# Second cross-attention: plain float32 matmuls, row maximum and sum on TensorE, another order of the batches

## The reference

```
x = x + tanh(g_xattn[0]) * L0_xattn(layernorm(x), ctx, ctx)
x = x + tanh(g_ffn[0])   * L0_ffn(layernorm(x))
x = x + tanh(g_xattn[1]) * L1_xattn(layernorm(x), ctx)
x = x + tanh(g_ffn[1])   * L1_ffn(layernorm(x))
```

```
Sim = (hc @ w1)[:, :, None] + (hq @ w2)[:, None, :] + einsum('bid,bjd->bij', hc * w3, hq) + b_sim
A = softmax(Sim, axis=2)
hq_hat = einsum('bij,bjd->bid', A, hq)
Batt = softmax(max(Sim, axis=2), axis=1)
hc_bar = einsum('bi,bid->bd', Batt, hc)[:, None, :]
feats = concatenate([hc, hq_hat, hc * hq_hat, hc * hc_bar], axis=-1)
out = feats @ W_qv + b_qv
```

## Time and profile before

| | us |
|---|---|
| median of 3 runs | 1298.6 |
| lowest, highest | 1297.71, 1306.02 |
| the profiled execution | 1298.1 |
| its span | 1296.2 |

### The profile page before, as it was taken

How to read it: one execution, slowest core, us unless ns; L and a number is a source line. 1 busy time by engine, 2 the same in 40 slices (tenths; PEclk the granted TensorE clock), 3 DMA queues, 4 the chain that set the end, 5 groups by cost and what they waited for, 6 DMA issues and landing times.

```text
span 1296.2 us, 22004 instructions
## 1 busy us (share of the span) xinstructions
PE 1076.1 (83%) x7088; PEld 931.2 (72%) x7088; DVE 869.5 (67%) x2028; ACT 508.4 (39%) x984; POOL 365.9 (28%) x391
## 2 busy tenths in 40 slices
PE   3478888697999999999999999835667998799930
PEld 3467777576888888888888888725567777588820
DVE  6779999967766776677667776755546567533323
ACT  5568888652333333333333333243232332122210
POOL 6345656432111111111001111142331222332235
PEclk9789999999999999999999999967887999899975
DMA  8920000010000000000000002110100520123224
GB/s 237 219 43 1 0 0 0 2 50 13 26 24 24 24 24 24 17 19 24 24 24 24 24 24 53 33 33 17 33 17 1 221 88 1 34 89 91 82 83 135
DMA packets 28388, 61.74 MB, mean 48 GB/s; under 512 B 4688, under 2 KB 13392, under 8 KB 28208
## 3 DMA queue, kind: packets, MB, share of 16 engines
q1 hardware_dynamic: 24928, 51.77, 13.3%
q0 software_dynamic: 3408, 9.31, 2.7%
HBM read 42.85 MB, written 9.31 MB: 40 GB/s over the span
## 4 chain that ended last, share of the span: by engine, by line
PE 63%; DVE 18%; issue 9%; POOL 3%; DMA 3%; ACT 2%; SPq 1%; DVEq 0%; POOLq 0%; ACTq 0%
PE bank L776 27%; PE bank L793 14%; PE bank L1153 6%; DVE ptl L570 3%; PE bank L1174 3%; DVE nmax L562 2%; PE bank L1091 2%; PE bank L380 2%; DMA yg<-y_rows,slot 1%; SPq L2077 1%; PE bank L1658 1%; POOL yg L1464 1%; DVE stats L681 1%; PE bank L1107 1%; DVE x L919 1%
## 5 line engine op out<-in xcount | busy, mean ns | idle before, releaser
L919 DVE SCALAR_TENSOR_TENSOR x<-bank,cw,x 128x256 f32<-128x256 f32 x528 | 218.1, 476 | 4.7 <-PE bank L793 4.7
L776 PE MATMUL bank<-xh,wh 128*128 128x512 f32 x528 | 207.8, 394 | 0.0
L776 PE MATMUL bank<-xl,wh 128*128 128x512 f32 x528 | 207.4, 393 | 0.0
L776 PE MATMUL bank<-xh,wl 128*128 128x512 f32 x528 | 206.0, 390 | 0.0
L995 POOL TENSOR_TENSOR wl<-wraw,wh 128x768 fp32r<-128x768 f32 x33 | 60.9, 1847 | 445.7 <-ACT wh L845 445.7
L865 ACT ACTIVATE hidh<-hid 128x512 fp32r<-128x512 f32 x132 | 83.4, 632 | 211.9 <-DVE hid L930 208.9
L793 PE MATMUL bank<-wh,hidh 128*128 128x256 f32 x528 | 150.4, 285 | 12.0 <-POOL hidl L1005 6.8
L793 PE MATMUL bank<-wh,hidl 128*128 128x256 f32 x528 | 150.5, 285 | 0.0
L793 PE MATMUL bank<-wl,hidh 128*128 128x256 f32 x528 | 150.5, 285 | 0.0
L936 DVE TENSOR_TENSOR hidl<-hid,hidh 128x512 fp32r<-128x512 f32 x124 | 85.9, 693 | 86.6 <-ACT hidh L865 86.6
L858 ACT ACTIVATE sil<-bank 128x512 f32<-128x512 f32 x132 | 79.0, 599 | 163.7 <-PE bank L776 163.7
(11 more groups left out here) (253 smaller groups left out, 2261.2 us busy)
## 6 DMA issues: line engine op xcount, KB each, us to landing
wraw<-in_w SPq DMA_DIRECT2D x37, 384.0 KB, 3.0
kst<-khl SPq DMA_DIRECT2D x32, 224.0 KB, 5.5
wres<-in_w SPq DMA_DIRECT2D x4, 1536.0 KB, 13.9
y_rows<-yb SPq DMA_DIRECT2D x39, 128.0 KB
x<-in_x SPq DMA_DIRECT2D x4, 512.0 KB, 6.2
craw<-in_ctxt SPq DMA_DIRECT2D x4, 512.0 KB, 4.2
traw<-in_ctx SPq DMA_DIRECT2D x4, 512.0 KB, 4.0
xn_rows<-xn SPq DMA_DIRECT2D x4, 512.0 KB, 11.6
```

The source lines that it names most:

```text
L776: mm = pe.matmul(o[:, :], wp[:, par, w], xp[:, c, b * SEQ:(b + 1) * SEQ], start=(n == 0), stop=(n == 5))
L919: op = nc.vector.scalar_tensor_tensor(out=x[:, t, :], in0=bank[4 + 2 * vp + j // 2][:, (j % 2) * DIM:(j % 2 + 1) * DIM], scalar=w, in1=x[: ...
```

## The change

It has four parts. First, the matmuls of the stage take float32 operands as they are: no high and low parts, a third of the matmuls, and ScalarE copies what comes out of PSUM once (`probs_copy`, `attended_copy`). Second, the two all-reduces go. The column of maxima is transposed by TensorE into one row (`maxima_row`), VectorE takes its maximum, and a matmul with a row of ones spreads it over the partitions (`maximum_spread`); a matmul with a matrix of ones makes the sum on all partitions (`sum_spread`). Third, the context and the tokens get two buffers each, the order of the steps on TensorE, ScalarE and VectorE is another one, and the output is made in halves of which each uses one bank. Fourth, the parameters and the routed weights get places in SBUF of which the stage uses none, and `load_routed1` issues the loads of `wres` before the stage.

```diff
--- before.py
+++ after.py
         def sync_a1(sp):
             sp.wait_ge(moe.up, 4 * NB0)
             for b in range(BATCH):
-                if b:
-                    sp.wait_ge(A["clo"], b)
-                sp.dma_start(craw[:, :, :], ctxt_in[:, :, b * SEQ:(b + 1) * SEQ]).then_inc(A["ctx_t"], 16)
-                if b:
-                    sp.wait_ge(A["tlo"], b)
-                sp.dma_start(traw[:, :, :], ctx_in[:, b * TPB:(b + 1) * TPB, :]).then_inc(A["ctx"], 16)
+                if b >= 2:
+                    sp.wait_ge(A["sim"], 4 * (b - 1))
+                sp.dma_start(craw[:, b % 2], ctxt_in[:, :, b * SEQ:(b + 1) * SEQ]).then_inc(A[f"ctx_t{b % 2}"], 16)
+                if b >= 2:
+                    sp.wait_ge(A["hq"], 2 * (b - 1))
+                sp.dma_start(traw[:, b % 2], ctx_in[:, b * TPB:(b + 1) * TPB, :]).then_inc(A[f"ctx{b % 2}"], 16)
...
             def scores(b, tiles):
...
                     for c in range(CH):
-                        for ap_, cp in ((aench, ctxh), (aench, ctxl), (aencl, ctxh)):
-                            mm = pe.matmul(bank[j % 2][:, :], ap_[:, c, j * P:(j + 1) * P], cp[:, c, :],
-                                           start=(k == 0), stop=(k == 5))
-                            k += 1
+                        mm = pe.matmul(bank[j % 2][:, :], aenc[:, b % 2, c, j * P:(j + 1) * P], craw[:, b % 2, c, :],
+                                       start=(c == 0), stop=(c == CH - 1))
                     mm.then_inc(A["sim"], 1)
...
+            def maxima_row(b):
+                pe.wait_ge(A["mx"], b + 1)
+                pe.wait_ge(A["enc"], min(2 * b + 4, 2 * BATCH))
+                pe.transpose(bank[3][0:1, 0:P], mx1[:, 0:1], ident).then_inc(A["mxt"], 1)
+
+            def maximum_spread(b):
+                pe.wait_ge(A["gmx"], b + 1)
+                pe.matmul(bank[3][:, P:P + 1], ones[0:1, :], gmx1[0:1, 0:1], start=True, stop=True).then_inc(A["gmb"], 1)
+
+            def sum_spread(b):
+                pe.wait_ge(A["eb"], b + 1)
+                pe.wait_ge(A["ngmx"], b + 1)
+                pe.matmul(bank[3][:, P + 1:P + 2], ones[:, :], ebs[:, 0:1], start=True, stop=True).then_inc(A["ebt"], 1)
...
             for b in range(BATCH):
-                probs_transposed(b, (0, 1))
                 if b + 1 < BATCH:
                     scores(b + 1, (0, 1))
+                if b == 0:
+                    maximum_spread(0)
+                probs_transposed(b, (0, 1))
+                if b == 0:
+                    sum_spread(0)
                 context_bar(b)
+                if b + 1 < BATCH:
+                    scores(b + 1, (2,))
                 probs_transposed(b, (2, 3))
                 if b + 1 < BATCH:
-                    scores(b + 1, (2, 3))
+                    scores(b + 1, (3,))
                 if b + 2 < BATCH:
                     transposes(b + 2)
                 attended(b)
...
         def pool_a1(pool):
...
-            def row_max(b):
-                pool.wait_ge(A["mx"], b + 1)
-                nc.gpsimd.partition_all_reduce(gmx1[:, :], mx1[:, :], P, RMAX).then_inc(A["gmx"], 1)
-
-            def row_sum(b):
-                pool.wait_ge(A["eb"], b + 1)
-                nc.gpsimd.partition_all_reduce(ebt[:, :], ebs[:, :], P, RADD).then_inc(A["ebt"], 1)
...
             parameters_a1(sp)
+            load_routed1(sp)
             sync_a1(sp)
```

More of the change, by code:

```diff
@@ L115, in gated_xattn_moe_kernel @@
         onesb = sb("onesb", [P, P], BF16)
-        ones8 = sb("ones8", [P, E1], F32)
+        ones = sb("ones", [P, P], F32)
         count = sb("count", [P, 161], F16)
@@ L1035, in constants_pool @@
                                     channel_multiplier=-1).then_inc(s_made, 1)
-            nc.gpsimd.memset(ones8[:, :], 1.0).then_inc(s_made, 1)
+            nc.gpsimd.memset(ones[:, :], 1.0).then_inc(s_made, 1)
             nc.gpsimd.iota(count[:, :], [[1, 161]], base=0, channel_multiplier=0,
@@ L1466, in moe1_pool, with load_routed1 @@
                         in_offset=bass.IndirectOffsetOnAxis(ap=slot[:, t, k:k + 1], axis=0)).then_inc(r1_yg[t % CG], 16)
+        def load_routed1(sp):
+            wv = w1_in.rearrange("e p c -> p e c")
+            for q in range(4):
+                sp.dma_start(wres[:, 4 * q:4 * q + 4, :], wv[:, SH1 + 4 * q:SH1 + 4 * q + 4, :]).then_inc(r1_wl, 16)
         def moe1_sync(sp):
@@ L1484, in moe1_sync @@
             load(1)
-            for q in range(4):
-                sp.dma_start(wres[:, 4 * q:4 * q + 4, :], wv[:, SH1 + 4 * q:SH1 + 4 * q + 4, :]).then_inc(r1_wl, 16)
             store_xn(0)
@@ L1689, in attended @@
                 for c in range(CH):
-                    k = 0
+                    if c == 1 and b + 1 < BATCH:
+                        maxima_row(b + 1)
                     for jc in range(TPB):
                         if c == 0:
-                            pe.wait_ge(A["ptl"], 4 * b + jc + 1)
-                        for tp, pp in ((tokh, p1th), (tokh, p1tl), (tokl, p1th)):
-                            mm = pe.matmul(bank[6 + c][:, :], tp[:, jc, c * P:(c + 1) * P], pp[:, jc, :],
-                                           start=(k == 0), stop=(k == 11))
-                            k += 1
+                            pe.wait_ge(A["pts"], 4 * b + jc + 1)
+                        mm = pe.matmul(bank[6 + c][:, :], traw[:, b % 2, jc, c * P:(c + 1) * P], p1t[:, jc, :],
+                                       start=(jc == 0), stop=(jc == TPB - 1))
@@ L1698, in attended @@
                     mm.then_inc(A["hq"], 1)
             def output(b):
-                pe.wait_ge(A["elo"], b + 1)
-                pe.wait_ge(A["wlo"], b + 1)
-                for j0 in (0, 2):
-                    for g, (fh, fl) in enumerate(((ench[:, b % 3], encl[:, b % 3]), (hqh, hql), (prodh, prodl))):
-                        if g and j0 == 0:
-                            pe.wait_ge(A["hql" if g == 1 else "prl"], 2 * b + 2)
-                        for j in (j0, j0 + 1):
-                            k = 0
-                            for c in range(CH):
-                                for fp, wp in ((fh, wqh), (fh, wql), (fl, wqh)):
-                                    mm = pe.matmul(bank[4 + j % 2][:, (j // 2) * DIM:(j // 2 + 1) * DIM], fp[:, c, j * P:(j + 1) * P],
-                                                   wp[:, CH * g + c, :], start=(g == 0 and k == 0),
-                                                   stop=(g == 2 and k == 5))
-                                    k += 1
-                            if g == 2:
-                                mm.then_inc(A["o"], 1)
+                if b + 1 < BATCH:
+                    maximum_spread(b + 1)
@@ new lines, in output @@
+                pe.wait_ge(A["w14"], b + 1)
+                for half in range(2):
+                    for g, feats in enumerate((enc[:, b % 3], hq, prod)):
+                        if g and half == 0:
+                            pe.wait_ge(A["hqs" if g == 1 else "prod"], 2 * b + 2)
+                        for j in (half, half + 2):
+                            for c in range(CH):
+                                w = wqv[:, CH * g + c, :] if g else w14[:, c, :]
+                                mm = pe.matmul(bank[4 + half][:, (j // 2) * DIM:(j // 2 + 1) * DIM],
+                                               feats[:, c, j * P:(j + 1) * P], w, start=(g == 0 and c == 0 and j == half),
+                                               stop=(g == 2 and c == CH - 1), skip_group_check=True)
+                    mm.then_inc(A["o"], 2)
+                    if half == 0 and b + 1 < BATCH:
+                        sum_spread(b + 1)
@@ L1829, in scalar_a1 @@
                     x_high(act, 1, 1)
-                if b + 1 < BATCH:
-                    tokens(b + 1)
-                if b + 2 < BATCH:
-                    encoder(b + 2)
-                    scaled_high(b + 2)
         def vector_a1(dve):
@@ L1983, in vector_a1 @@
                     ln_norm(dve, 3, 0, moe.xn)
+                residual(b, 0)
+                if b + 1 < BATCH:
+                    row_softmax(b + 1)
+                if b == BATCH - 2:
                     ln_norm(dve, 3, 1, moe.xn)
-                residual(b)
+                residual(b, 1)
                 if b + 2 < BATCH:
```

240 lines of the change are left out of this document (78 added, 162 removed), and 3 rows, old and new, of the table s_a1.

## The result

The changed kernel takes 1259.16 us (median of 4 runs, 1255.11 to 1263.34) against 1298.15 us of the kernel before (4 runs, 1293.68 to 1306.02): ratio 0.9694, 95% interval 0.9635 to 0.9752. The time lies in the range of 1247 to 1270; the gain is 39 us where 43.7 was worked out.

A forecast was written before the change was run, and what follows sets the result against it. Waits, not any engine's work, bound the stage, caused by GpSimd's switches around all-reduces. TensorE's 119.1 + 8.3 + 1.5 + 1.1 + 1.5 = 131.5 us against 175.2 gave 1298.6 - 43.7, 1255 us; range 1247 to 1270.

The forecast's parts named there:

- The price of plain float32: On TensorE, a plain matmul was taken at 0.865 us for 512 columns and 0.433 for 256, 97.0 us of new work.
- rival A: Plain float32 matmuls on TensorE cost 0.912 us for 512 columns, 0.480 for 256: 7.4 us more, 1262 us; chance 0.10.
- Worth nothing beyond the waits that they sat in: Removing ScalarE's and VectorE's splits in the stage was given no gain of its own, since neither engine was the bound.
- The start of the stage: From the first transposes at 842.1 us to the scores' end at 859: nothing gained, 8.3 us of TensorE time lost.
- Batch 0: 1.5 us counted: In the first batch the softmax chain from maximum to reciprocal isn't covered by an output; stall taken as 1.5 us.
- Rival E: The granted clock stays below 0.73 over the whole stage, making the kernel slower, 1374 us at 0.50; chance 0.02.
- The last batch: 1.1 us: With no scores ahead of them, the transposed probabilities wait for the second half of the residual: 1.1 us.
- 1.5 us for late semaphores: An allowance of 1.5 us in the stage's sum for late semaphores outside the start, first batch and last batch.
- The three small matmuls: Per batch on TensorE: maxima column transposed, maximum spread, sum spread, at 0.25 us each, 3.0 us in all.
- rival B: Small matmuls wait in TensorE's queue for VectorE or ScalarE, 3 us a batch, 12 us in all: 1267 us; chance 0.15.
- rival C: Moved weights give 3 us at the next expert stage and the missing start stall 2 us: 1250 us; chance 0.08.
- Every stretch after a stall begins there: In the kernel before, TensorE's granted clock was said to start at 0.50, the 1.2 GHz level, after each stall.

The follow-up runs named there:

- e5: The changed kernel with each matmul of the attended tokens made twice, with the same result: stage 162.0 us, 1288.19 us in one run.
- e1: The changed kernel with maximum and sum over partitions given back to GpSimd's all-reduces, plain float32 and new order kept: stage 140.3 us, 1263.04 us.
- e10: The kernel before, splits kept, with new order, TensorE's reductions and the encoder scaled from SBUF: stage 158.8 us, 1281.48 us.
- e9: The kernel before, splits and GpSimd's all-reduces kept, in the new order with the encoder scaled from SBUF: stage 181.4 us, 1306.13 us.
- e4: The changed kernel with three unused plain matmuls of 256 columns put into TensorE's 1.5 us wait in batch 0: stage 131.8 us, 1254.19 us.
- e7: The changed kernel with the old order of steps on TensorE and ScalarE: stage 134.4 us, 1258.09 us in one run.
- e8: The changed kernel with five all-reduces added on GpSimd whose result nobody uses: stage 133.2 us, 1256.5 us in one run.
- e2: The changed kernel with the routed experts' weights loaded in their old place, behind the stage: stage 135.1 us, 1258.43 us.
- e3: The changed kernel with steps reordered in the first and last batch so that TensorE's short waits go: stage 127.6 us, 1251.26 us.

## Why the prediction came out, point by point

- **The stage and its bound.** Right. 135.1 us where 131.5 was worked out; a batch took 29.35 us (29 to 30 said); the clock in the loop is 1.00; e5 shows TensorE as the bound.
- **The price of plain float32.** Right. The chain shows 8 records, which are four matmuls, and 24 records for twelve of 256 columns:

```profile
899.84 3.43 PE bank L1647 x8
...
918.40 5.38 PE bank L1712 x24
923.89 5.29 PE bank L1712 x24
```

  3.43 / 4 = 0.858 us (0.865 said), 5.29 / 12 = 0.441 us (0.433 said): rival A is false. The four passes of true FP32 that the Trainium skill names (FP8 and Floating Point Precision, TensorE Precision Notes) don't cost four split products here: 0.86 us against 0.91.
- **"Worth nothing beyond the waits that they sat in", said of ScalarE's and VectorE's splits, with GpSimd's switches as the cause.** This is the step that failed. The time came out because the change removes both, and the sum was made over what is left and not over what goes. As an account of the 40 us it was wrong: without splits the switches cost 5 to 10 us (e1), and without switches the kernel with splits is 23.7 us longer (e10). An engine that is busy for less than the bound can still be late: the chain through it decides, not its sum. How much of the 23.7 us is the single buffers' and the old output layout's, at most a few us by e10's waits, stays open. The 27.1 us in e9 are the two together.
- **The start of the stage.** Right in total: from the first transpose to the second batch's scores 17.0 us (847.55 to 864.56), as 842.1 to 859 said.
- **Batch 0: 1.5 us counted.** The term of the sum that was mis-sized: 35.1 − 29.35 = 5.75 us. The wait itself has the 1.5 us that were said; the clock at 0.66 behind it costs 3.3 more (e4), for which the sum had no term. Of the 0.9 left, 0.4 are two small matmuls that only this batch makes inside its own loop. Rival E looked for the clock over the whole stage, and not behind one short wait.
- **The last batch: 1.1 us.** The wait was 0.6; but its attended tokens took 8.27 us where 7.03 are normal (e7, e8), at a clock of 0.66 from 962 to 966 us. The batch begins at 957.49 and ends 25.2 us later; the sum has 22.5 of work and 1.1.
- **1.5 us for late semaphores** wasn't needed: in the two steady windows TensorE is busy for 40.00 of 40 us.
- **The three small matmuls** waited for nothing in the loop: rival B is false. The one wait of this kind is in batch 0 (1.2 us for `mx`, inside the 17.0 of the start). In the chain they take 0.11, 0.31 and 0.12 us, 2.2 in all four batches, where the sum has 3.0.
- **The moved weights, counted at nothing.** Right (e2); rival C is false.
- **1259 against 1255.** The stage accounts for 3.6 of the 4.3 us. It is a balance of misses: 4.2 too little in batch 0 and 1.6 in the last, against 1.5 too much for the semaphores and 0.8 for the small matmuls.
- **"Every stretch after a stall begins there", at 0.50.** Not every one: in the kernel before, TensorE waits 2.3 us ahead of the scores of the earlier trace rows at 856.48, and the clock is 1.00 through the wait and behind it.

## What to carry to other kernels

Work on engines that aren't the bound is free only if it isn't a link between two operations of the bound: before keeping a split "because the other engines have room", follow its chain from producer to matmul and see what stands ahead of each link on its queue. Two causes that stand in one line share their waits: removed one at a time they seem to be worth more than the two together (22.6 + 41.1 against 46.3), so test all four corners before crediting either. In a stage bound by TensorE look at the granted clock behind each short wait: the price of the wait may be three times its length, and either other ready work or an idle matmul in the gap takes it away. Compare two traces batch by batch before you believe a difference of 2 or 3 us: here the same code gave as much.

## What the runs showed of the hardware

- **A wait of 1.5 us cost 4.8.** TensorE had done transposes and small matmuls, waited 1.5 us, and did 16 one-column records; its clock, at full (2.4 GHz) from 860 to 870, then has a mean of 0.66 from 870 to 880, that is, partly at 1.2 GHz. With three unused matmuls in the wait it stayed at 1.00 (e4), and with a wait of 0.4 to 0.5 us at this place too (e3). In e2 and e8, where the wait of 1.5 us is unchanged, the four records of scores behind it take 3.76 us too. In the last batch a wait of 0.6 us before the same small matmuls was followed by 0.66 from 962 to 966, and likewise in e2 and e4; but in e5, e7 and e8 the same wait left the clock up, and so did the waits of 0.6 us in e7's loop. The length of a wait alone doesn't say whether the clock falls. The window of the changed kernel's last batch:

```profile
962.00:966.00 4.00, 4.00 (x9) 1.84 (x8) 1.84 (x9) 0.84 (x2) 1.27 (x2) 0.66 0.00 0
```

  TensorE is busy for all of it: busy time doesn't show that the work is slow.
- **The switch of GpSimd goes both ways and disturbs nobody.** 5.8 to 7.5 us between an all-reduce and an ordinary instruction in either direction (e1, e8, e9), put down to "issue": 5.8 to 6.6 ahead of an all-reduce, 6.5 to 7.5 on the way back. Two all-reduces with no ordinary instruction between them have none (in e8 the second starts 0.3 us after the first). In e8 TensorE's batches are no longer than in the change.
- **A plain float32 matmul costs 3.7 to 3.8 split products**: 0.86 us for 512 columns against 0.684 for three and 0.912 for four, and 0.441 for 256 columns against 0.360 and 0.480.
